# Three normalizations with features on partitions: variances by strip products, one root on 128x128, the MLP input without DMA

## The reference, cut to what matters

```python
def _layernorm(x, g, b):
    mu = jnp.mean(x, axis=-1, keepdims=True)
    var = jnp.mean(jnp.square(x - mu), axis=-1, keepdims=True)
    return (x - mu) * jax.lax.rsqrt(var + LN_EPS) * g + b
...
msg = msg.reshape(N, L, C) @ Wm
msg = _layernorm(msg, g1, b1)                  # norm 2
h = jnp.concatenate([x, msg], axis=-1) @ W1
h = jax.nn.relu(h) @ W2
msg = _layernorm(h, g2, b2)                    # norm 3
return x + msg
...
t = t + attn(_ln_t(t), ...)                    # norm 1 is this _ln_t
t = t + ffn(_ln_t(t), ...)                     # norm 4 is this _ln_t
```

## Time and profile before

| | |
|---|---|
| median of three runs | 1195.16 us (1192.1 to 1196.35) |
| profiled execution: time, span | 1201.06 us, 1199.2 us |
| PE busy | 1075.0 us, 90% |
| DVE, ACT, POOL busy | 783.8, 681.4, 359.3 us |
| chain that ended last | 68% PE, 16% DVE, 12% ACT |

### The profile page before, as it was taken

One profiled execution on the slowest core, in us unless ns is written; L12 is line 12 of the kernel. 1 busy time (PEld: TensorE's weight loads), 2 busy tenths in 40 slices (PEclk: granted clock), 3 DMA queues, 4 the chain that ended last, 5 costly groups with the idle time before them and its releaser, 6 DMA issues.

```text
span 1199.2 us, 15483 instructions
## 1 busy us (share of the span) xinstructions
PE 1075.0 (90%) x5863; PEld 497.3 (41%) x5878; DVE 783.8 (65%) x1673; ACT 681.4 (57%) x930; POOL 359.3 (30%) x277
## 2 busy tenths in 40 slices
PE   5888759989999899998999989998999989999898
PEld 2454526433554245442453424542354424534232
DVE  4764746588556975488655886659754887547434
ACT  2336345755755656665657656565566555676454
POOL 0100031244312433134322344123431342314465
PEclk9987889999999999999999999999999999999999
DMA  4010069006810095102940059100771019400580
GB/s 148 1 36 1 1 145 211 1 18 132 207 36 18 1 210 129 34 18 53 223 98 1 18 119 219 36 15 4 166 173 36 19 29 222 88 1 18 113 198 27
DMA packets 17418, 96.64 MB, mean 81 GB/s; under 512 B 3648, under 2 KB 6720, under 8 KB 13120
## 3 DMA queue, kind: packets, MB, share of 16 engines
q1 hardware_dynamic: 17344, 95.66, 34.5%
HBM read 77.82 MB, written 9.44 MB: 73 GB/s over the span
## 4 chain that ended last, share of the span: by engine, by line
PE 68%; DVE 16%; ACT 12%; issue 3%; SPq 1%; DMA 0%; DVEq 0%; POOL 0%; POOLq 0%; ACTq 0%
PE HP L809 14%; PE HP L794 12%; PE R L642 7%; PE R L729 5%; ACT H L942 5%; PE R L598 5%; PE R L587 4%; PE R L578 3%; DVE SM L1127 3%; PE R L660 3%; PE R L651 2%; PE R L736 2%; PE R L809 2%; DVE TM L1277 2%; ACT XB L887 1%
## 5 line engine op out<-in xcount | busy, mean ns | idle before, releaser
L988 POOL TENSOR_TENSOR XB<-TM,XB 128x512 f32<-128x512 f32 x254 | 321.3, 1287 | 670.4 <-DVE TM L1277 670.3
L942 ACT ACTIVATE H<-HP,W 128x1024 f32<-128x1024 f32 x224 | 237.6, 1113 | 112.3 <-PE HP L794 111.8
L794 PE MATMUL HP<-XF,W1E 64*128 64x512 f32 x1024 | 256.0, 618 | 24.3 <-DVE TM L1277 23.8
L1277 DVE SCALAR_TENSOR_TENSOR TM<-HP,B2S,CWB 128x512 f32<-128x512 f32 x224 | 161.5, 746 | 132.4 <-PE HP L809 129.1
L809 PE MATMUL HP<-H,W 128*64 128x512 f32 x896 | 226.4, 613 | 22.1 <-ACT H L942 22.1
L794 PEld LDWEIGHTS HP<-XF,W1E 64*128 64x128 f32 x1024 | 87.3, 185 | 148.1 <-DVE TM L1277 82.2
L876 ACT ACTIVATE T<-R 128x512 f32<-128x512 f32 x128 | 73.8, 598 | 101.5 <-PE R L642 89.0
L809 PEld LDWEIGHTS HP<-H,W 128*64 128x64 f32 x896 | 49.4, 135 | 170.6 <-ACT H L942 132.5
L1127 DVE TENSOR_REDUCE SM<-T 128x8 f32<-128x512 f32 x128 | 85.1, 684 | 29.5 <-ACT T L876 27.3
L1099 DVE SCALAR_TENSOR_TENSOR BIG<-R,T 128x512 f32<-128x512 f32 x112 | 70.2, 685 | 30.1 <-PE R L578 29.8
L598 PE MATMUL R<-W,T 128*128 128x128 f32 x512 | 73.4, 289 | 5.7 <-DVE T L1146 5.2
(11 more groups left out here) (165 smaller groups left out, 1363.9 us busy)
## 6 DMA issues: line engine op xcount, KB each, us to landing
CWB<-gates_hbm SPq DMA_DIRECT2D x32, 1536.0 KB, 22.0
CWB<-gates_hbm SPq DMA_DIRECT2D x32, 512.0 KB, 10.0
BIG<-XN SPq DMA_DIRECT2D x32, 256.0 KB, 4.5
out<-XB SPq DMA_DIRECT2D x15, 512.0 KB, 2.9
X<-x SPq DMA_DIRECT2D x14, 512.0 KB, 7.8
W<-wpack SPq DMA_DIRECT2D x1, 1064.0 KB, 5.0
XF<-x SPq DMA_DIRECT2D x2, 512.0 KB, 6.2
gates_hbm<-CWR SPq DMA_DIRECT2D x16, 64.0 KB, 1.6
```

The costliest lines, as they stand in the source:

```text
L794: last = mm(HP[u % BATCH][:, half(k)], W1E[img(k), e, :], XF[img(k), 1 - par, s, half(c)], start=True, stop=True)
L942: f(activated(b, u).rearrange("p k t -> p (k t)"), HP[u % BATCH][:, :], ACT.Gelu, bias=col(B1E + e))\
L988: nc.gpsimd.tensor_tensor(acc, TM[:, u % BATCH, :], acc, ALU.add).then_inc(acc_done, 1)
L1277: v.scalar_tensor_tensor(out=TM[:, u % BATCH, :], in0=sums_of(b, u), scalar=B2S[:, e % 2, e // 2:e // 2 + 1], in1=CWB[:, s, e, half(c)], o ...
```

## The change

Norms 2, 3 and 4 keep the features on the partitions. The centring product is now `by_feature`, one product of 512 columns per piece. ACT squares it into `T2` and also copies the centred values themselves into `T1` (`kept`). `variance` multiplies the squares with `LINES`, a matrix that sums 64 partitions into one output row; by the choice of its columns each block of 128 tokens gets rows of its own, and the four pieces write four strips of 32 partitions: 16 products of 128 columns with 32 weight columns. The variances of a whole group then stand on one 128x128 tile, and `root` makes the reciprocal roots there in nine operations. `spread` multiplies each strip with `SPAN` (32 rows, 128 weight columns), which puts a token's root on all 64 of its partitions: again 16 products of 128 columns. DVE multiplies that with the copy (`scaled`), for the message in `T1`, for norm 3 in `T1` and then with b2 into `XB`, for norm 4 straight into `XF`, the experts' input.

The MLP product is split: `W1X` times the features straight from `XN` and `W1G` times the normalized message from `T1`, each with 64 rows, added in PSUM; `U` and its transfers are gone. b2 moves from ACT's `XB` pass into the third norm, and POOL makes `XB` from `XN` and the convolution's result. `LINES`, `SPAN`, `W1X`, `W1G` and `G1S` are set up in the opening, by 14 more transfers and three more fills, and `prepare` on DVE waits for six of these transfers. The gate weights' tile `CWR` becomes part of `RT`. Both `SCHEDULE` and `OPENING` are written anew.

```diff
-    ("message.0", ""), ("message.1", ""), ("rstd_2", ""), ("norm_2.0", ""), ("norm_2.1", "HY"),
-    ("features_2.0", ""), ("features_2.1", ""), ("hidden_0.0", ""), ("hidden_0.1", ""), ("hidden_1.0", ""),
...
+    ("message.0", ""), ("message.1", "H"), ("variance_2", ""), ("rstd_2", "Y"), ("spread_2", ""),
+    ("norm_2.0", ""), ("norm_2.1", "H"), ("hidden_0.0", "Y"), ("hidden_0.1", ""), ("hidden_1.0", ""),
...
-        U = [[BIG[:, s, k, :] for k in range(2)] for s in range(G)]
...
+        ROOTS = BIG[:, 0, 0, 0:4 * P].rearrange("p (k t) -> p k t", k=4)
...
+            w1 = wpack[:, COLS["w1"][0]:COLS["w1"][0] + HID]
+            for k in range(2):
+                sp.dma_start(W1X[img(k), :], w1[img(0), :]).then_inc(w1_in, 16)
+                sp.dma_start(W1G[img(k), :], w1[img(1), :]).then_inc(w1_in, 16)
+                sp.dma_start(G1S[img(k), :], wpack[img(1), COLS["cols"][0] + G1:COLS["cols"][0] + G1 + 2]).then_inc(w1_in, 16)
+            spans = reps[:, NREP * P:(NREP + NQ) * P].rearrange("p (n c) -> p n c", c=P)
+            for i in range(len(PIECES)):
+                sp.dma_start(SPAN[32 * i:32 * i + 16, :, :], spans[0:16, :, :]).then_inc(span_in, 16)
+                sp.dma_start(SPAN[32 * i + 16:32 * i + 32, :, :], spans[32:48, :, :]).then_inc(span_in, 16)
...
-                def attention_input(slots):
-
-                    for s in slots:
-                        sp.wait_ge(num_ps[s], at(a + 1, LAST))
-                        for k in range(2):
-                            sp.dma_start(U[s][k][0:C, :], XN[img(k), s, :]).then_inc(u_in[s], 16)
-
...
+                def by_feature(s, c, src, weights):
+
+                    return mm(R[s][:, half(c)], weights, src[:, s, half(c)], start=True, stop=True)
...
+                def variance(k):
+
+                    if starting(a):
+                        pe.wait_ge(lines_set, 3)
+                    for s in range(G):
+                        pe.wait_ge(ln_sq[s], at(a * LNS + k, LAST))
+                    pe.wait_ge(cp_done, copies(k) + 1)
+                    for q in range(NQ):
+                        lines = LINES[:, 2 * (NQ - 1 - q):2 * (NQ - 1 - q) + 32]
+                        for i, (s, c) in enumerate(PIECES):
+                            last = mm(R[G - 1][32 * i:32 * i + 32, CH:CH + P], lines, T2[:, s, some_tokens(c, q)],
+                                      start=(q == 0), stop=(q == NQ - 1))
+                    last.then_inc(var_ps, 1)
+
+                def spread(k):
+
+                    if starting(a):
+                        pe.wait_ge(span_in, 16 * 2 * len(PIECES))
+                    pe.wait_ge(rs_done, a * (LNS - 1) + k - 1)
+                    pe.wait_ge(cp_done, copies(k) + len(PIECES))
+                    for q in range(NQ):
+                        for i, (s, c) in enumerate(PIECES):
+                            rows = slice(32 * i, 32 * i + 32)
+                            last = mm(R[s][:, some_tokens(c, q)], SPAN[rows, q, :], ROOTS[rows, 3, :], start=True, stop=True)
+                            if q == NQ - 1:
+                                last.then_inc(ln_back[s], 1)
 
                 def one_everywhere(s, c):
 
@@ -627,7 +667,7 @@
...
-                        by_token(s, c, T2, WMC[:, :]).then_inc(ln_ps[s], 1)
-
-                def hidden(k, slots):
-                    for s, c in pieces(slots):
-                        if k == 0:
-                            pe.wait_ge(u_in[s], a * 32 + 32)
-                            pe.wait_ge(msg_norm[s], at(a + 1, c))
+                        by_feature(s, c, T2, WMC[:, :]).then_inc(ln_ps[s], 1)
+
+                def hidden(c, slots):
+                    for s in slots:
+                        if c == 0:
+                            pe.wait_ge(msg_norm[s], at(a + 1, LAST))
                         else:
-                            pe.wait_ge(h_done[s], at(a * 2 + 1, c))
-                        mm(R[s][:, half(c)], W1G[:, :], U[s][k][:, half(c)], start=True, stop=True)\
-                            .then_inc(h_ps[s], 1)
+                            pe.wait_ge(h_done[s], at(a * 2 + 1, LAST))
+                        for k in range(2):
+                            mm(R[s][:, half(k)], W1X[img(k), :], XN[img(k), s, half(c)], start=True, stop=False)
+                        for k in range(2):
+                            mm(R[s][:, half(k)], W1G[img(k), :], T1[img(k), s, half(c)], start=False, stop=True)\
+                                .then_inc(h_ps[s], 1)
 
...
+                def centred(k, slots):
+
                     for s, c in pieces(slots):
                         act.wait_ge(ln_ps[s], at(a * LNS + k, c))
                         f(T2[:, s, half(c)], R[s][:, half(c)], ACT.Square).then_inc(ln_sq[s], 1)
+                        if (s, c) == PIECES[-1]:
+                            kept(k, s, c)
+
+                def kept(k, s, c):
+
+                    f(T1[:, s, half(c)], R[s][:, half(c)], ACT.Copy, scale=col(G2) if k == 3 else 1.0).then_inc(cp_done, 1)
+
+                def variance(k):
+                    for s, c in PIECES[:-1]:
+                        kept(k, s, c)
...
-                        f(XN[:, s, half(c)], R[s][:, half(c)], ACT.Copy)
-                        if c == 0 and exists(a - 2):
-                            act.wait_ge(out_done[s], a * 16 - 16)
-                        f(XB[:, par, s, half(c)], R[s][:, half(c)], ACT.Identity, bias=col(B2)).then_inc(xb_part[s], 1)
...
-                        f(U[s][0][C:P, half(c)], R[s][img(0), half(c)], ACT.Copy)
-                        f(U[s][1][C:P, half(c)], R[s][img(1), half(c)], ACT.Copy).then_inc(msg_norm[s], 1)
...
+                        f(XN[:, s, half(c)], R[s][:, half(c)], ACT.Copy).then_inc(xn_back[s], 1)
...
-                        pool.wait_ge(xb_part[s], at(a + 1, LAST))
+                        pool.wait_ge(xn_back[s], at(a + 1, LAST))
+                        if exists(a - 2):
+                            pool.wait_ge(out_done[s], a * 16 - 16)
                         source = convolution_buffers(a)[0]
-                        nc.gpsimd.tensor_tensor(XB[:, par, s, :], XB[:, par, s, :], source[:, s, :], ALU.add)\
+                        nc.gpsimd.tensor_tensor(XB[:, par, s, :], XN[:, s, :], source[:, s, :], ALU.add)\
...
+                dve.wait_ge(w1_in, 6 * 16)
...
+                def root(k):
+
+                    dve.wait_ge(var_ps, a * (LNS - 1) + k - 1)
+                    h, g, t, y = (ROOTS[:, i, :] for i in range(4))
+                    link(v.tensor_scalar(h, R[G - 1][:, CH:CH + P], 0.5 * LN_EPS, None, ALU.add))
+                    link(v.tensor_scalar(y.bitcast(I32), h.bitcast(I32), -0.5, RSQRT_GUESS, ALU.mult, ALU.add))
+                    link(v.tensor_tensor(g, h, y, ALU.mult))
+                    link(v.tensor_tensor(t, g, y, ALU.mult))
+                    link(v.scalar_tensor_tensor(out=t, in0=t, scalar=-5 / 3, in1=t, op0=ALU.add, op1=ALU.mult))
+                    count(v.scalar_tensor_tensor(out=g, in0=t, scalar=1.25, in1=g, op0=ALU.add, op1=ALU.mult))
+                    link(v.scalar_tensor_tensor(out=y, in0=t, scalar=1.25, in1=y, op0=ALU.add, op1=ALU.mult))
+                    link(v.tensor_tensor(t, g, y, ALU.mult))
+                    v.scalar_tensor_tensor(out=y, in0=t, scalar=-2 / 3, in1=y, op0=ALU.add, op1=ALU.mult).then_inc(rs_done, 1)
 
...
+                def scaled(k, s, c, dst):
+
+                    dve.wait_ge(ln_back[s], at(a * LNS + k, c))
+                    return v.scalar_tensor_tensor(out=dst, in0=R[s][:, half(c)], scalar=ROOT_SCALE, in1=T1[:, s, half(c)],
+                                                  op0=ALU.mult, op1=ALU.mult)
+
+                def scale_message(s):
...
+                        scaled(2, s, c, T1[:, s, half(c)]).then_inc(msg_norm[s], 1)
+
+                def scale_hidden(s):
+                    for c in range(NCH):
+                        scaled(3, s, c, T1[:, s, half(c)]).then_inc(y3_done[s], 1)
+                    dve.wait_ge(xs_done[s], a + 1)
+                    for c in range(NCH):
+                        dve.wait_ge(y3_done[s], at(a + 1, c))
+                        v.scalar_tensor_tensor(out=XB[:, par, s, half(c)], in0=T1[:, s, half(c)], scalar=col(B2),
+                                               in1=XB[:, par, s, half(c)], op0=ALU.add, op1=ALU.add)\
+                            .then_inc(x2_done[s], 1)
+
+                def scale_input(s):
+                    for c in range(NCH):
+                        scaled(4, s, c, XF[:, par, s, half(c)]).then_inc(xf_done[s], 1)
 
                 def elu_plus_one(n, dst, slots):
```

137 lines of the change are left out of this document (62 added, 75 removed), and 52 rows, old and new, of tables (OPENING, SCHEDULE).

## The result

The changed kernel takes 1211.2 us (median of 4 runs, 1210.4 to 1211.5) against 1193.9 of the kernel before (1192.1 to 1196.4); the ratio on record is 1.0138, 95% interval 1.0121 to 1.0155. It is slower; the forecast was faster, 1186. The time lies within the range of 1170 to 1213, but it moved the other way.

A forecast was written before the change was run, and what follows sets the result against it. TensorE was taken as the bound, busy for 130.4 us of a 141 us period. Message to gates -2, query -9 and opening +2 gave -9, so 1186 us from the median of 1195.2; 8-in-10 range 1170 to 1213.

The forecast's parts named there:

- TensorE's own work: TensorE's products per group: 25.5 us removed, 23.5 added, so 2.0 us less; the other end is +5.4.
- V and S: Added variance and spreading products, 16 instructions of 128 columns each: 1.18 and 1.30 us, three times per group, 7.4 together.
- The rival of records: Packed variance and spreading products priced by records, not columns: 1244 us in full, 1215 half way; chance 0.15.
- Message to gates: Stretch from message to gates: waits 4.1 us against 1.9 now; net -0.3 per period, -2 us over 7 groups.
- the root becomes the bound: Rival at spreads 2 and 3: they wait the whole 2.9 us of the root, +27, 1212 us; chance 0.10.
- The query: Query's 1.40 us wait for ScalarE's XN and XB passes: -1.5 us per period, -9 us in six groups.
- hidden anyway: Rival: the query's wait moves to the next batch waiting for VectorE, only opening effects are left, 1194 us; chance 0.15.
- Router stages and replication keep their work: Router and replication stretch: VectorE's 25.3 busy of 27.5 us sets the pace; 0, with -1 to +1 per period.
- the prediction's own sign of being wrong: On TensorE: packed records above 45 ns, or an unlisted wait above 1 us per period, would refute the prediction.
- The opening: Opening up to group 0's gates: +4.5 from late `prepare`, -2.5 from hidden layer to gates, together +2 us.
- Late weights: Opening: `prepare` waits for six transfers behind SPREAD's, first replication near 23.9 us, VectorE's work 4 to 5 later, +4.5.
- The baseline: Start of the sum: the runs' median of 1195.2 us, 5.9 below the profiled execution's time of 1201.1.

The follow-up runs named there:

- e7: Kernel before with ScalarE writing only XN after the first features and GpSimd making XB from XN plus the input, b2 left out: 1185.3 us, ratio 0.9939.
- e9: Changed kernel with the old order from channel_stats to centre_1, in key/value and in the opening, and early hidden-layer weight transfers: 1189.2 us, ratio 0.9940.
- e12: Kernel before with the changed kernel's order of stages and batches from channel_stats to conv_out and kv_turn to numerator: 1209.5 us, ratio 1.0126.
- e4: Changed kernel with the six transfers for the hidden layer's weights issued ahead of the pads wait and SPREAD's sixteen: 1208.2 us, ratio 1.0124.
- e1: Changed kernel with choose_2 and gate_rows ahead of the next group's rstd_1, norm_1.1 and features_1.1 in the opening: 1206.2 us, ratio 1.0108.
- e13: Kernel before, unchanged, profiled again in a single execution: 1196.5 us.
- e14: Kernel before, unchanged, profiled a third time in a single execution: 1192.7 us.
- e3: Changed kernel with the key/value stages (kv_turn, kv_values, denominator, numerator) in the order of the kernel before: 1202.8 us, ratio 1.0085.
- e8: Changed kernel without the last three of the root's nine steps in the three norms that use it: 1194.6 us, ratio 1.0011.
- e15: e9 with next high_1.1 moved beside norm 3's root and next high_1.0 behind its scalings in the opening: 1188.0 us, ratio 0.9944.

## Why the prediction was wrong

- **TensorE's own work: right in sign, 1.8 us too small.** In a window it is 126.6 instead of 130.4, -3.8 for the forecast -2.0; the added products overlap at their ends (the hidden layer's 7.3 us for 8.0, the wide centring products' 7.7 for 8.1, V and S 6.8 for 7.4). V takes 1.08 us and S 1.17 for the forecast 1.18 and 1.30. The rival of records is false: 32 records of 128 columns in 1.08 us are 34 ns each, below the 73 that no row before undercut, so columns set the price. The Trainium skill (TensorE: Matmul & The Clock Gate, section "Wait — 56ns, not 53.3ns?") has a floor of 62 ns per matmul with hardware decode off; by it V would take 2.0 us, an estimate, and this trace doesn't show that floor.
- **Message to gates: right.** Spreads 0.96 and 0.97 for 1.0, spread 4 none, its second batch 0.36 for 0.3, centring 4 0.70 and 0.54 for 0.35 and 0.6, the gates 0.73 for 0.8. TensorE's idle time went from 1.9 to 4.3 us there, for the forecast 4.1. Net -0.7 for -0.3. The rival that the root becomes the bound asked for 2.9 us at two spreads, three times what they wait.
- **The query: right**, -1.5 per period in the changed kernel and -1.46 alone (e7); it didn't move to the next batch, so the rival "hidden anyway" is false.
- **"Router stages and replication keep their work; the batches are moved by one or two places ...: 0" failed.** Moving them by one place left one batch, not two, between the mask products and the first replication, which waits for the copy of the gates' rows: +1.5 us per period (e9 and e12). This is also the prediction's own sign of being wrong, a wait that it doesn't list, above 1 us per period. For key and value products the sum had no term at all, though the diff turns the slots round there: +1.0. Together with small shifts that is the 2.3 us per period between the changed kernel and e9; over the six full periods 14 us. "0, with -1 to +1" rested on VectorE's busy share alone (25.3 of 27.5 us). VectorE did keep its pace; the step that failed is from there to TensorE: I didn't lay out what stands ahead of the copy in VectorE's queue and how much work TensorE has beside it.
- **The opening: the term was named, the place that cost most wasn't.** Late weights were forecast at +4.5 and cost 2 to 3 (e4). The order of choose_2 and gate_rows behind the next group's norm wasn't counted: +5 (e1; 3.6 by the ratios). The stretch from hidden layer to gates, forecast at 26 to 28, took 27 (121.8 to 148.8).
- **The baseline failed.** I took the 5.9 us between the profiled execution and the median over to the changed kernel. They belong to the opening of the kernel before, whose length varies (e13, e14); the changed kernel doesn't show it, its four runs lie within 1.2 us, those of the kernel before within 4.3. That is 6 us.
- **Sum.** 1186 + 14 + 5 + 6 = 1211, what was measured. It closes better than its terms deserve: the late weights cost 2 us less than forecast, and the mechanisms that held gave 0.2 us more per period, so some 3 us of the loss have no named place. That 1211 lies in the range is luck: the range reached so high for packed records (1215) and for the root as the bound (1212), and neither happened. With the order restored (e9) the period is 138.9, 2.0 below before, for the forecast 1.8. The mechanisms that were forecast hold; the loss is in edits to the order that I priced at nothing, and in the baseline.

Shown are the order in the steady state (e3, e9, e12), its part in the opening (e1), the query (e7), the root (e8) and the varying opening (e13, e14). The norms are 0.6 us per period to the good in e9, and yet it gains no more than e7 (0.9940 against 0.9939). Between the two profiled executions, whose openings are about equally long (gates at 146.3 and 145.1), the gain is there: spans of 1186.7 and 1188.8, 2.1 us apart, which is six periods of 0.57 less the 1.2 at the gates. But e7's runs reach down to 1182.2 us (1182.2 to 1190.6) and e9's lie at 1188.5 to 1190.1. That e7's faster runs are those with a short opening, as in e13 and e14, fits, but those runs have no trace. Why the changed opening stays at the long end is open: that its norms have no cover was only argued, and e15 didn't bear it out.
